# Straight v projection, a projected rotary partner for the first chunk, and a new order of uses and stores in an axial-attention and state-space kernel

## The reference

```python
an = _ln(a, ga, ba); bn = _ln(a, gb, bb)
q = an @ Wq
k, v = jnp.split(bn @ Wkv, 2, axis=-1)
q = _rope(q, sin, cos); k = _rope(k, sin, cos)      # x*cos + rotate_every_two(x)*sin
attn = jax.nn.softmax(jnp.einsum('bhid,bhjd->bhij', q, k), axis=-1)
out = jnp.einsum('bhij,bhjd->bhid', attn, v)        # then heads interleaved
return jax.nn.elu(out @ Wo + bo)
...
return x + (xi + xj) / 2
```

## Time and profile before

| | |
|---|---|
| median of 3 runs | 334.65 us (333.85 to 337.41) |
| the profiled execution | 336.71 us, its span 334.6 us |
| TensorE matmul busy | 235.9 us (70%), weight loads 142.4 us |
| VectorE busy | 203.9 us (61%) |
| ScalarE busy | 171.3 us (51%) |
| GpSimd busy | 126.9 us (38%) |
| mean granted TensorE clock | 0.879 |
| scores of unit 0 start / of unit 14 start | 23.79 us / 136.35 us |

### The profile page before, as it was taken

How to read it: one execution, slowest core, us unless ns; L and a number is a source line. 1 busy time by engine, 2 the same in 40 slices (tenths; PEclk the granted TensorE clock), 3 DMA queues, 4 the chain that set the end, 5 groups by cost and what they waited for, 6 DMA issues and landing times.

```text
span 334.6 us, 7775 instructions
## 1 busy us (share of the span) xinstructions
PE 235.9 (70%) x3138; PEld 142.4 (43%) x3138; DVE 203.9 (61%) x333; ACT 171.3 (51%) x298; POOL 126.9 (38%) x104
## 2 busy tenths in 40 slices
PE   0366776886749694674259669998999867976453
PEld 0143444554425453452248335653444434445312
DVE  2668668684635453347535495899786868285333
ACT  2142554577553737183533674367447644933282
POOL 1411669114615160550040087367496971400000
PEclk9999798999996969597556989999799997997758
DMA  7510010433030303410354300000000000002002
GB/s 191 207 63 33 33 66 32 109 84 82 16 96 0 90 10 64 94 36 0 73 112 91 75 18 0 2 5 3 0 4 2 0 2 2 0 3 65 0 1 63
DMA packets 34243, 15.26 MB, mean 46 GB/s; under 512 B 31008, under 2 KB 31520, under 8 KB 34080
## 3 DMA queue, kind: packets, MB, share of 16 engines
q1 hardware_dynamic: 32480, 13.67, 16.1%
q10 hardware_dynamic: 1728, 1.10, 1.2%
HBM read 5.42 MB, written 2.10 MB: 22 GB/s over the span
## 4 chain that ended last, share of the span: by engine, by line
PE 38%; DVE 22%; ACT 17%; issue 11%; DMA 5%; SPq 5%; POOL 1%; ACTq 1%; DVEq 0%; POOLq 0%
PE ring L565 17%; PE score L565 8%; PE oz L565 4%; DMA rot_swap<-rot_sin 4%; PE ring L570 3%; PE p_turn L565 3%; SPq L537 3%; SPq L524 2%; DVE ln_v L864 2%; PE p_turn L570 2%; DVE mix L1142 2%; DVE ln_s L844 2%; ACT prob_t L1302 2%; DVE xhat L879 2%; DVE rot_sin L1006 2%
## 5 line engine op out<-in xcount | busy, mean ns | idle before, releaser
L1527 POOL TENSOR_TENSOR a_msk<-dt_fin,c_sb 128x512 f32<-128x512 f32 x32 | 39.7, 1239 | 34.4 <-DVE dt_fin L981 22.6
L1302 ACT ACTIVATE prob_t<-p_turn 128x512 f32<-128x512 f32 x32 | 17.7, 595 | 41.9 <-PE p_turn L570 41.8
L565 PE MATMUL score<-k_bd,q_rot 32*64 32x128 f32 x512 | 23.0, 330 | 17.6 <-POOL q_rot L895 16.0
L1142 DVE TENSOR_TENSOR mix<-dec,g_m 128x512 f32<-128x512 f32 x32 | 31.4, 987 | 2.2 <-ACT dec L1384 1.5
L1047 DVE TENSOR_REDUCE s_max<-score 128x16 f32<-128x1024 f32 x16 | 19.5, 1221 | 20.7 <-PE score L565 20.7
L1006 DVE SCALAR_TENSOR_TENSOR rot_cos<-ring,b_att,p_sb 128x512 f32<-128x512 f32 x15 | 11.2, 747 | 30.2 <-PE ring L565 17.2
L570 PE MATMUL ring<-c_sb,xhat 128*128 128x128 f32 x44 | 11.1, 401 | 25.1 <-DVE xhat L879 21.3
L565 PEld LDWEIGHTS score<-k_bd,q_rot 32*64 32x64 f32 x512 | 18.2, 165 | 23.5 <-POOL q_rot L895 18.2
L565 PE MATMUL score<-a_msk,c_sb 128*128 128x512 f32 x44 | 25.2, 656 | 0.0
L895 POOL TENSOR_TENSOR q_rot<-rot_cos,rot_swap 128x512 f32<-128x512 f32 x7 | 8.9, 1266 | 42.3 <-DMA rot_swap<-rot_sin 42.3
L1512 POOL TENSOR_TENSOR dtx<-xv,dt_fin 64x512 f32<-64x512 f32 x16 | 19.8, 1239 | 13.2 <-PE p_turn L565 12.2
(11 more groups left out here) (177 smaller groups left out, 582.6 us busy)
## 6 DMA issues: line engine op xcount, KB each, us to landing
rot_swap<-rot_sin SPq DMA_DIRECT2D x32, 128.0 KB, 2.1
p_sb<-params SPq DMA_DIRECT2D x1, 1520.0 KB, 9.2
x_tok<-x SPq DMA_DIRECT2D x16, 64.0 KB, 2.5
attention_j_turned<-y_tok SPq DMA_DIRECT2D x16, 64.0 KB, 2.2
back<-attention_j_turned SPq DMA_DIRECT2D x16, 64.0 KB, 2.4
ut_a<-u SPq DMA_DIRECT2D x8, 126.0 KB, 2.8
ut_b<-u SPq DMA_DIRECT2D x8, 124.0 KB, 3.1
ut_b<-u SPq DMA_DIRECT2D x8, 122.0 KB, 3.2
```

Of the source, the lines that this page charges most:

```text
L565: return pe.matmul(dst, lhsT, rhs, start=start, stop=stop, skip_group_check=True)
L1142: v.tensor_tensor(mix[:, e % LAPS, :, :], dec[:, e % LAPS, :, :], wide(g_m[:, e // 4 % 2, e % 4, :], SSM_H), ALU.mult)\
L1302: a.activation(prob_t[:, e % 2, 4 * hp:4 * hp + 4, :].rearrange("p k n -> p (k n)"), PT[hp], ACT.Identity)\
L1527: gp.tensor_tensor(a_msk[:, m % LAPS, :, :], deep(dt_fin[:, 0, SSM_H * m:SSM_H * (m + 1)], GRID), wide(cst("tri"), SSM_H), ALU.mult).then_ ...
```

## The change

v is projected with the tokens as the stationary operand, so that it comes out in key rows at once: `v_sb`, its copy, the `vt` transposes and their waits go. In direction j that is 8 matmuls, in direction i 32 small ones. v's bias is left off and enters as `b Wo` in the output bias (`bo`, two one-column matmuls and two small additions). For chunk 0 a second projection with pair-swapped weights (`qs`, `ks`) takes the place of the partition-swapping DMA. The k of chunk 1 gets its projection ahead of the first scores, in the banks of `p_turn`. The uses move: q(g+1) to even step 2g, then v(g) and `yt`; k(g+2) and `wo(g-2)` to odd step 2g+1. SyncE issues both swaps of a chunk ahead of the stores of `y_tok`. `fold` and the late weights move four steps later, and the layer norms of the first steps are ordered anew.

```diff
-    steps = {-1: ([("xr", 0), ("k", 0), ("q", 0), ("xr", 1), ("v", 0), ("vt", 0)], [], [])}
+    steps = {-1: ([("xr", 0), ("k", 0), ("q", 0), ("v", 0), ("xr", 1), ("k", 1)], [], [])}
...
+        if n == 1:
+            a, b, c = [], [], [("xr", 2), ("k", 2)]
         elif n == 2:
-            a, b, c = [("vt", 1), ("q", 2)], [("v", 2)], [("k", 3)]
+            a, b, c = [], [("q", 2)], [("v", 1), ("xr", 3)]
+        elif n == 3:
+            a, b, c = [], [("k", 3)], [("bo", 0)]
         elif odd:
-            a, b, c = [("vt", g + 1)], [("q", g + 2)], []
+            a, b, c = [("wo", g - 2)] if g - 2 < ATT_CHUNKS - 1 else [], [("k", g + 2)], []
         else:
-            a, b, c = [("wo", g - 2)], [("v", g + 1)], [("k", g + 2), ("yt", g - 3)]
+            a, b, c = [("wo", g - 2)] if g - 2 == ATT_CHUNKS - 1 else [], [("q", g + 1)], [("v", g), ("yt", g - 3)] if n else []
...
-FOLD_STEP = 4
+FOLD_STEP = 8
...
-            for g in range(CHUNKS):
+            for g in range(1, CHUNKS):
                 swap(g, 0)
                 swap(g, 1)
...
             for g in range(CHUNKS):
                 swap(CHUNKS + g, 0)
+                swap(CHUNKS + g, 1)
                 sp.wait_ge(y_turned, g + 1)
...
-                swap(CHUNKS + g, 1)
...
+                elif kind == "v" and d == 0:
+                    for k in range(2):
+                        for a in range(2):
+                            for u in range(2):
+                                last = mm(half_of(use, u)[:, DIM * (2 * k + a):DIM * (2 * k + a) + DIM],
+                                          xn_cols(0, c, u, a)[:, P * k:P * k + P], weight(w_att[d][64 * u:64 * u + 64, :], d, "v"))
+                elif kind == "v":
+                    for u in range(2):
+                        for k in range(2):
+                            for a in range(2):
+                                for m in range(2):
+                                    for r in range(2):
+                                        row = 64 * m + 32 * r
+                                        last = mm(half_of(use, u)[row:row + 32, DIM * (2 * k + a):DIM * (2 * k + a) + DIM],
+                                                  xn_i[64 * r:64 * r + 64, 16 * c + 8 * u + 4 * k + 2 * a + m, :],
+                                                  weight(w_att[d][64 * r:64 * r + 64, :], d, "v"))
...
-            ln_vector_a(v, 0)
-            v.wait_ge(xa_in[1], 32)
-            ln_mean(v, 1)
             ln_vector_b(v, 0)
-            ln_centre(v, 1)
             ln_vector_c(v, 0)
...
             for use in att_steps[-1]:
                 att_use(use)
+                if use == ("k", 0):
+                    k_sum(v, 0)
+                    ln_vector_c(v, 1)
                 if use == ("q", 0):
-                    ln_vector_b(v, 1)
-                    ln_vector_c(v, 1)
-                    v.wait_ge(xa_in[2], 32)
-                    ln_vector_a(v, 2)
-                    k_sum(v, 0)
-                    v.wait_ge(k_added, 1)
-                    k_mask(v, 0, 1)
                     q_sum(v, 0)
...
-            copy_xn(0)
+            gp.memset(v_bd[:, :, :, :], 0.0).then_inc(v_zeroed, 1)
             gp.wait_ge(mid_in, 16)
             scale_weights(1)
-            gp.memset(v_bd[:, :, :, :], 0.0).then_inc(v_zeroed, 1)
+            copy_xn(0)
```

More of the change, by code:

```diff
@@ L135, in ring_plan @@
         kind = use[0]
-        if use == ("q", 0):
+        if use in (("q", 0), ("k", 1)):
             banks = ()
@@ L139, in ring_plan @@
             banks = (0, 1)
-        elif kind in ("xr", "vt", "wo", "yt", "fold"):
+        elif kind in ("xr", "wo", "yt", "fold", "bo"):
             banks = (2,)
@@ L219, in build @@
         y_t = sb("y_t", [P, 2, CHUNKS, CW])
-        sin_s = [sb("sin_s0", [P, GRID]), sb("sin_s1", [P, CW])]
-        w_att = [sb(f"w_att{d}", [P, 3 * DIM]) for d in range(2)]
-        b_att = sb("b_att", [P, 6])
+        sin_s = [sb("sin_s0", [P, CW // 2]), sb("sin_s1", [P, CW])]
+        w_att = [sb(f"w_att{d}", [P, len(WEIGHTS[d]) * DIM]) for d in range(2)]
+        b_att = sb("b_att", [P, 8])
+        bo_v = sb("bo_v", [P, 2])
         w_xdt = sb("w_xdt", [P, INNER + SSM_H])
@@ L457, in pair_of @@
         def pair_of(use):
-            return score if use == ("q", 0) else ring
+            return {("q", 0): score, ("k", 1): p_turn}.get(use, ring)
         def middle(use):
@@ L576, in biases @@
             def biases(d):
-                for k, which in enumerate(("ba", "bb", "bb")):
-                    for m in range(2):
-                        rows = slice(64 * m, 64 * m + 64)
-                        last = mm(oz[rows, 3 * d + k:3 * d + k + 1], par("wqkv_" + "ji"[d])[rows, DIM * k:DIM * k + DIM],
-                                  col(which + "_" + "ji"[d])[rows, :])
+                w = par("wqkv_" + "ji"[d])
+                for name in WEIGHTS[d]:
+                    at = BIASES[d] + WEIGHTS[d][name]
+                    b = col(("ba_" if name in ("q", "qs") else "bb_") + "ji"[d])
+                    for m in range(2 if name != "v" else 0):
+                        rows = slice(64 * m, 64 * m + 64)
+                        last = mm(oz[rows, at:at + 1], weight(w, d, name)[rows, :], b[rows, :])
+                if d == 1:
+                    for e in range(2):
+                        at = BIASES[e] + WEIGHTS[e]["v"]
+                        last = mm(oz[:, at:at + 1], par("v_wide_" + "ji"[e])[0:64, :], col("bb_" + "ji"[e])[0:64, :])
                 last.then_inc(bias_made, 1)
@@ L619, in att_use @@
                     last = turn(dst, xhat[:, g % 2, :])
-                elif kind == "vt":
-                    pe.wait_ge(v_copied, g + 1)
-                    last = turn(dst, v_sb[:, :])
+                elif kind == "bo":
+                    pe.wait_ge(mid_in, 16)
+                    pe.wait_ge(bias_here, 2)
+                    for d in range(2):
+                        at = BIASES[d] + WEIGHTS[d]["v"]
+                        last = mm(dst[:, d:d + 1], par("wo_" + "ji"[d]), b_att[:, at:at + 1])
                 elif kind == "wo":
@@ L706, in _ @@
                 att_use(use)
-                if use == ("vt", 0):
+                if use == ("v", 0):
                     pe.wait_ge(mid_in, 16)
@@ L1285, in _ @@
             for use in att_steps[-1]:
[L1286 removed]
+                if use == ("k", 0):
                     ln_scalar_a(a, 1)
                     ln_scalar_b(a, 1)
[L1289 to L1290 removed]
                     a.wait_ge(consts_in, 16)
                     a.wait_ge(k_added, 1)
[L1293 to L1294 removed]
+                    for r in range(2):
+                        a.activation(k_bd[:, 0, r, :], k_rot[:, :], ACT.Identity, scale=cst("head_mask")[:, r:r + 1]).then_inc(k_ready, 1)
+                if use == ("xr", 1):
+                    att_use(use)
+                    att_use(("v", 0))
+                elif use != ("v", 0):
+                    att_use(use)
             for n in range(ATT_STEPS):
```

149 lines of the change are left out of this document (88 added, 61 removed).

## The result

| | before | after |
|---|---|---|
| median beside each other | 335.07 us (333.85 to 337.41) | 316.66 us (313.90 to 319.39, four runs) |
| ratio | | 0.937, interval 0.928 to 0.946 |
| the profiled execution, its span | 336.71, 334.6 us | 319.39, 317.3 us |
| scores of unit 0, unit 14; transposes of unit 15 | 23.79, 136.35; 148.52 us | 21.25, 118.94; 130.92 us |
| TensorE matmul busy, mean granted clock | 235.9 us, 0.879 | 231.5 us, 0.893 |

The change makes the kernel 6.3% faster, and the median is 0.3 us from the forecast. The executions after the change fall into two pairs 5 us apart; a ratio compares the quicker executions of the two kernels and a median takes all (which is why 316.66 / 335.07 is not 0.937), and the profiled execution is of the slower pair.

A forecast was written before the change was run, and what follows sets the result against it. Bound: the chain through SyncE's queue, the q swap behind `y_tok` stores, in attention's second half. Profiled 336.71 less 19.8 gives 316.9; the median lies 2.1 lower, 314.8; plus 2 us allowance, 317 us. Range 308 to 329.

The forecast's parts named there:

- The gain at the end of attention: Transposes of unit 15, where layer one's attention ends: forecast at 128.7 us against 148.5 before, a gain of 19.8 us.
- The ramp: First steps up to unit 4: scores of unit 0 at 21.1 us, unit 4 at 49.8 against 56.66, gain 6.9 us.
- Direct v: Direction i's v on TensorE, 32 matmuls of 64 columns in the even step: 1.0 us, with ends 0.8 and 1.9.
- v(0): Chunk 0's v on TensorE ahead of unit 0's scores: taken as 2.0 us, between bounds of 1.1 and 3.6.
- units 8 to 10: Stretch with the fold waiting for `yt`'s copy, 1.9 us more, and the late scales, 0.9: forecast 13.9 us.
- The hole of unit 8: TensorE's wait ahead of unit 8, whose q sum comes late behind the `x_tok` loads: some 3 us left.
- Direct v is dear: Rival: direction i's v takes 1.9 us, not 1.0, costing 0.95 on each of four chunks: 321 us; chance 0.17.
- A smaller hole stays: Rival: scores of units 10, 12, 14 and the end still wait some 2.5 us for q: 327 us; chance 0.19.
- Only a shuffle: Rival: the first steps give half the booked gain and holes stay: 331 to 334 us, no measurable change; chance 0.05.
- Half clock everywhere: Rival: TensorE stays at 1.2 GHz throughout, a chunk takes 18.9 us, the kernel is slower at 358 us; chance 0.06.
- The hand-over: End of attention into layer two: the `back` loads, ready 124 to 133 us, first asked for at 129 to 143, stay hidden.
- The last term: Allowance of 2 us added to the median for waits and turnarounds that a schedule laid by hand forgets.

## Why the prediction was right, point by point

**The bottleneck.** "In the second half of the attention the path runs through SyncE's queue": shown from both sides. Moving that one line in the kernel before takes 23 us off, and moving it back in the kernel after brings three holes.

**The gain at the end of attention.** Forecast 19.8 us, measured 17.6 (148.52 - 130.92); outside that stretch nothing changed between these two profiles (188.2 us before, 188.5 after). The sum for the profiled execution, 316.9, was 2.5 low for 319.39.

**Its terms.** Starts forecast and measured: unit 0 21.1 and 21.25, unit 2 36.3 and 36.57, unit 4 49.8 and 50.16, unit 8 77.0 and 77.95, unit 10 90.9 and 94.15, unit 12 104.1 and 106.85, unit 14 116.4 and 118.94, the end 128.7 and 130.92. The ramp was right to half a microsecond, with xhat at 8.6 (forecast 8.3), k rotated at 14.9 (14.75) and q at 17.6; that is in part luck, since other profiles of the same ramp start unit 0 some 2 us earlier (last section). Direct v took 1.10 us (1.0), v(0) 1.97 (2.0). The term mis-sized was units 8 to 10, 13.9 forecast and 16.2 measured. (Its own terms, 12.3 and 1.9, make 14.2; where the other 0.3 went it does not say.) The layout was right for full clock: the kernel with the loads spread needs 15.4 us at a clock of 1.00, of which 1.6 are the late weights without their cover, and that leaves 13.8. What I left out is that the hole of unit 8, which I had forecast, brings the lower clock after it (0.76 in this stretch), as three of the four holes of before did: the scores of unit 8 take 1.99 us and the transposes behind them 1.97, each 0.9 over full clock. A second slow piece, `wo` and unit 8's transposes from 88.8 to 92.4 us with 1.91 each, comes after seven microseconds at full clock. It goes with the hole (the kernel with the loads spread has clock 1.00 there, with the same wait of 1.36 us ahead of the fold), but what brings it was not found. The later chunks came out 0.5 and 0.2 shorter than laid out. The fold's wait and matmuls, booked at 1.9, were 1.95; the late weights, "up to 3" without cover, were 1.6.

**The hole of unit 8.** Right in place and cause: q sum forecast at 27.1 of those two chunks, the scores 27.8 after unit 4. The run with the loads spread shows the cause, the block of `x_tok`. The hole was 4.5 us, not some 3.

**The rivals.** *Direct v is dear* fell: 1.10 us, not 1.9. The trace does not bear out the rule on which it rested, the Trainium skill's that row tiles cannot use one PSUM bank at the same time (TensorEngine Tiling (Array Packing), "Gotcha 1: PSUM Pressure"): in turn the row groups took 1.10 us, one after the other 1.79. *A smaller hole stays* fell beyond unit 8: q had 1.9 us to spare on paper, and the waits of the scores for it are gone from unit 10 on. *Only a shuffle* fell: the ramp gave 6.5 us of the 6.9 booked (56.66 - 50.16), and the holes beyond unit 8 went. *Half clock everywhere* fell: granted clock 1.00 from unit 10 to the transposes of unit 15, in spite of a wait ahead of every v.

**The hand-over.** "Hidden, with little slack at the first" held, with more slack: GpSimd had the four parts of `back` ready at 125.8, 129.1, 131.8 and 134.9 us, and VectorE took the first at 134.5, after a wait for TensorE and not for GpSimd.

**What the forecast didn't ask.** It read a chunk without its hole as 11.3 us and laid out the new one at 12.3, and never drew the conclusion: of the change's parts the queue order earns everything in the steady chunks, and v behind the rotation gives some of it back. The median was met because the costs of the other parts had been put into the layout, not because the parts had been priced apart. The last term, 2 us of allowance over the median, covered the mis-sized one by luck: none of the four executions came nearer to 317 than 1.8 us.

## What to carry to other kernels

SyncE's queue issues in the order of its list (the k swap of chunk 4 went out at 68.21 us, 0.1 after the last of 16 loads): when a transfer that somebody waits for stands behind a wait or a block of others that nobody needs yet, move it first and alone, and time that by itself; here it was worth as much as the whole change. Spread a block of loads (11.6 us of issuing here) between the latency-critical ones. When a projection is moved, look at the ring bank it takes: it should not be one whose reader is the slowest piece of the same step, and each extra piece (here the fold) belongs where its reader's turn comes early.

## What the runs showed of the hardware that was not expected

Two row groups of the array that write the same PSUM bank in alternate matmuls overlap (1.10 us for v of a chunk, where two at a time would take at least 1.92 by the estimate above, and 1.79 when not alternated); all four chunks of direction i show the same pair.

The same code differs between executions. From the last transposes of `xhat` to the end of the span, layer two took 149.0 us after the change (from 168.29 to 317.3) and 144.5 with the stores first again (172.97 to 317.5), though it is the same program there; the other profiles lie near one or the other (144.6 with the moved fold, 147.7 to 149.3 elsewhere). Unit 0's scores started at 21.25 us after the change and at 19.20 with the stores first again, for the same instructions ahead of them. The traces show where: v of chunk 0 takes 1.97 us in the one and, in the other,

```profile
14.80 1.11 PE L584 MATMUL ring<-w_att,xn_j 64*128 64x64 f32 x16 [0.27 <-DVE rot_swap L1070]
```

and the small bias products behind it take 1.53 and 0.93 us, the next transposes of `xhat` 1.11 and 0.66. That is TensorE at its lower and its higher speed, although the column of the granted clock reads 1.00 in both from 15 to 17 us: the durations tell more than the column there. What decides when TensorE gets faster at the start, and what makes layer two quicker, was not tried; a single profile is therefore good for stretches, and not for the sum, to better than 5 us.
